# Two destinations in one sum of the count table: weights 1 and 256, and one 16-bit copy for two bytes

## The reference, cut to what matters

```python
pooled = jax.ops.segment_sum(h[col], row, num_segments=N)       # first network, 2 layers
agg    = jax.ops.segment_sum(h[src], dst, num_segments=N)       # second network, 4 layers
agg    = agg / jnp.maximum(deg, 1.0)[:, None]
aggregated = jax.ops.segment_sum(messages, receivers, num_segments=n_nodes)
```

## Time and profile before

| what | value |
|---|---|
| median of 3 runs | 3236.5 us (3234.55 to 3239.82) |
| the profiled execution's span | 3240.8 us |
| TensorE busy | 2943.5 us (91%), mean granted clock 0.951 |
| VectorE busy | 1047.2 us (32%) |
| ScalarE busy | 729.8 us (23%) |
| GpSimd busy | 1114.7 us (34%) |

### The profile page before, as it was taken

How to read it: one execution, slowest core, us unless ns; L and a number is a source line. 1 busy time by engine, 2 the same in 40 slices (tenths; PEclk the granted TensorE clock), 3 DMA queues, 4 the chain that set the end, 5 groups by cost and what they waited for, 6 DMA issues and landing times. The chain is left out here.

```text
span 3240.8 us, 44117 instructions
## 1 busy us (share of the span) xinstructions
PE 2943.5 (91%) x18657; PEld 1740.9 (54%) x18657; DVE 1047.2 (32%) x1860; ACT 729.8 (23%) x1173; POOL 1114.7 (34%) x1012
## 2 busy tenths in 40 slices
PE   1799969997899869999999999999899877999998
PEld 1688835553444335555555555554355664555554
DVE  5899922223200261211111111113311483222122
ACT  4799912223100230000000000001100383011000
POOL 5000013330000004562562663664167101553564
PEclk6899979998999979999999999999899987999999
DMA  7133599994466226666665665664566213665665
GB/s 260 50 129 129 163 244 173 164 170 89 120 147 146 44 66 206 178 171 169 177 175 165 182 178 163 173 173 121 146 181 179 78 54 101 176 180 161 171 170 156
DMA packets 768367, 492.61 MB, mean 152 GB/s; under 512 B 362500, under 2 KB 749836, under 8 KB 767568
## 3 DMA queue, kind: packets, MB, share of 16 engines
q1 hardware_dynamic: 705362, 395.76, 50.5%
q0 software_dynamic: 30112, 62.69, 6.6%
q10 hardware_dynamic: 32702, 31.44, 3.1%
HBM read 334.89 MB, written 76.82 MB: 127 GB/s over the span
## 5 line engine op out<-in xcount | busy, mean ns | idle before, releaser
L2159 PE MATMUL acc<-tbuf,hs 128*128 128x448 fp8e4 x8232 | 1602.0, 354 | 20.0 <-PEq L1242 8.8
L2136 POOL DMA_INDIRECT grow<-hrows,glist x882 | 940.6, 1066 | 791.9 <-PE acc L2183 388.3
L2159 PEld LDWEIGHTS acc<-tbuf,hs 128*128 128x128 f16 x8232 | 801.2, 98 | 762.9 <-issue 52.5
L2298 DVE TENSOR_TENSOR edge_loc<-iota,gdl 128x768 f16<-128x768 bf16 x147 | 140.6, 971 | 743.9 <-PE acc L2183 714.4
L731 PE MATMUL quad<-K,S 128*128 128x196 bf16 x1568 | 278.0, 250 | 17.6 <-DVE K L655 17.6
L1627 PE MATMUL acc<-tbuf,hs 128*128 128x512 fp8e4 (+1 forms) x1300 | 279.6, 369 | 14.9 <-DMA tbuf<-table 14.9
L711 ACT ACTIVATE stage<-quad 128x784 fp8e4<-128x784 f32 x392 | 287.4, 838 | 11.6 <-PE quad L731 5.8
L735 PE MATMUL deg<-K,S 128*128 128x196 bf16 x1568 | 276.8, 248 | 0.0
L1500 PE MATMUL acc<-tbuf,hs 128*128 128x512 fp8e4 (+1 forms) x1300 | 267.4, 369 | 0.7 <-issue 0.7
L2267 ACT ACTIVATE H<-B,vectors 128x448 f32<-128x448 f32 (+2 forms) x56 | 37.4, 668 | 820.3 <-DVE B L2338 820.3
L1500 PEld LDWEIGHTS acc<-tbuf,hs 128*128 128x128 f16 x1300 | 123.6, 98 | 144.4 <-issue 4.3
(11 more groups left out here) (301 smaller groups left out, 2008.5 us busy)
## 6 DMA issues: line engine op xcount, KB each, us to landing
tbuf<-table SPq DMA_DIRECT2D x294, 448.0 KB, 3.6
tbuf<-table SPq DMA_DIRECT2D x294, 336.0 KB, 3.2
table<-stage SPq DMA_DIRECT2D x6, 5488.0 KB, 19.4
grow<-hrows,glist POOLq DMA_INDIRECT x882
hrows<-hs SPq DMA_DIRECT2D x28, 448.0 KB, 4.4
feat<-in_edge_attr_dram ACTq DMA_DIRECT2D x27, 448.0 KB, 6.6
C<-factors ACTq DMA_DIRECT2D x2, 3136.0 KB, 12.5
table<-stage SPq DMA_DIRECT2D x2, 2744.0 KB, 12.2
```

Source lines behind the costliest of these rows:

```text
L2136: g.indirect_dma_start(out=grow[:, n % 2, t, :], out_offset=None, in_=k.hrows[l % 2], in_offset=bass.IndirectOffsetOnAxis(k.glist[:, i // ...
L2159: mm = T.matmul(acc(s, h), rows[l % 2][:, g * US + r, part, :], counts[:, (r - lo) * STRIP + h * HALF:(r - lo) * STRIP + (h + 1) * HALF], ...
L2298: V.tensor_tensor(hot[:, n % 2, :, :], k.iota[:, 0:P].unsqueeze(1).to_broadcast([P, GH, P]), k.gdl[:, i // GU, i % GU * GH:(i % GU + 1) * ...
```

## The change

One sum holds two destinations. A window still has four destinations, but a key now has only two places per block of sources (WU = 2, so NKEY falls from 196 to 98). The lower bit of the destination goes into the weight instead: an edge to an even destination adds 1, one to an odd destination adds 256. So S is no longer a plain one-hot array but a weighted one, and it is written with one instruction per window, which reads two numbers per partition (`win_low` and `win_odd`) as its scalar operands. A sum below 65536 is copied as one 16-bit integer, whose two bytes are the two counts, eight windows per copy. Read as 8-bit floats, the bytes 0 to 15 stand for the count times 2^-9 (CODE), and the scales by which the sums are multiplied take that back. The degrees and the check for large counts take the two bytes apart first. The core of the diff:

```diff
-NKEY = NS * WD
+WU = WD // 2
+NKEY = NS * WU
+ODD = 256.0
+CODE = 2.0 ** -9
-NQUAD = NBATCH * NBW // 4
+NWE = 8
+NOCT = NBATCH * NBW // NWE
...
# first_stage, windows(n)
-                    V.tensor_scalar(high[at], both[:, :, :, 0], 7, None, ALU.logical_shift_right)
+                    V.tensor_scalar(high[at], both[:, :, :, 0], 6, 0xFFFE, ALU.logical_shift_right, ALU.bitwise_and)
+                    V.tensor_scalar(junk[at].bitcast(I32), both[:, :, :, 1], 1, None, ALU.bitwise_and)
...
-                    V.scalar_tensor_tensor(loc[:, 1, g0:g1, :], high[at], float(WD), dl[at], ALU.mult, ALU.add
+                    V.scalar_tensor_tensor(loc[:, 1, g0:g1, :], dl[at], 1.5, high[at], ALU.is_ge, ALU.add
                                            ).then_inc(loc_ok.h, 1)
+                    V.tensor_scalar(loc[:, 2, g0:g1, :], junk[at].bitcast(I32), ODD - 1.0, 1.0, ALU.mult, ALU.add
+                                    ).then_inc(loc_ok.h, 1)
...
# build_tables, VectorE
-                        hot(S[:, q, :, :], k.iota[:, 0:SRC_W], k.win_low[:, at, :], NBW, SRC_W)
+                        for i in range(NBW):
+                            w = u * NBW + i
+                            V.tensor_scalar(S[:, q, i, :], k.iota[:, 0:SRC_W], k.win_low[:, w:w + 1],
+                                            k.win_odd[:, w:w + 1], ALU.is_equal, ALU.mult)
                         hot(K[:, q, :, :], k.iota[:, 0:NKEY], k.win_key[:, at, :], NBW, NKEY).then_inc(hots.h, 1)
...
-                V.tensor_reduce(degl[:, :], deg[:, 0:2 * NKEY].rearrange("p (h b d) -> p b h d", h=2, d=WD), AXY, ALU.add
+                V.tensor_copy(packed[:, :], deg[:, 0:2 * NKEY]).then_inc(split_ok.h, 1)
+                dve.wait_ge(split_ok.h, split_ok.at(1))
+                V.tensor_scalar(bytes_of[:, 0, :], packed[:, :], 255, None, ALU.bitwise_and)
+                V.tensor_scalar(bytes_of[:, 1, :], packed[:, :], 8, None, ALU.logical_shift_right).then_inc(split_ok.h, 1)
+                dve.wait_ge(split_ok.h, split_ok.at(2))
+                V.tensor_tensor(summed[:, :], bytes_of[:, 0, :], bytes_of[:, 1, :], ALU.add).then_inc(split_ok.h, 1)
+                V.tensor_tensor(many[:, :], bytes_of[:, 0, :], bytes_of[:, 1, :], ALU.max).then_inc(split_ok.h, 1)
+                dve.wait_ge(split_ok.h, split_ok.at(4))
+                V.tensor_reduce(degl[:, :], summed[:, :].rearrange("p (h b d) -> p b h d", h=2, d=WU), AXY, ALU.add
                                 ).then_inc(deg_ok.h, 1)
+                V.tensor_reduce(verdict[:, 1:2], summed[:, :], AX, ALU.add).then_inc(judge.h, 1)
...
# build_tables, ScalarE: 196 copies of eight windows in place of 392 of four
-                            stage[:, b, :, to:to + 4 * WD].rearrange("p b (w d) -> p w b d", d=WD),
+                            pairs16[:, b, :, to:to + NWE * WU].rearrange("p b (w d) -> p w b d", d=WU),
...
# build_tables, TensorE: both products of a window are 98 columns wide
+                            mm = T.matmul(pair[o % 3][:, at:at + NKEY], S[:, q, i, :], K[:, q, i, :],
...
# layer_chain, TensorE, ahead of layer 0
+                if conv:
+                    pe.wait_ge(own_ok.h, own_ok.at(2 * L))
...
# layer_chain, VectorE, at the place of L2370
-                if conv:
-                    V.tensor_scalar(own[1][:, :], layers[1][0], scale(0, 1), None, ALU.mult).then_inc(own_ok.h, 1)
+                for l in range(L if conv else 0):
+                    for i in range(2):
+                        V.tensor_scalar(own[l][i], layers[l][0], scale(0, l), (CODE, 1.0)[i], ALU.mult, ALU.mult
+                                        ).then_inc(own_ok.h, 1)
```

More of the change, by code:

```diff
@@ L10 @@
 I32 = mybir.dt.int32
+U16 = mybir.dt.uint16
 ALU = mybir.AluOpType
@@ L567, in lists @@
                 def lists(m):
-                    g0, g1 = WHALF[m // 2]
+                    g0, g1 = WHALF[m // 3]
                     act.wait_ge(loc_T.h, loc_T.at(2 + m))
[L570 to L574, removed]
+                    at = turned[(m + 1) % 4][:, 0:(g1 - g0) * P]
+                    if m % 3 == 0:
+                        return k.win_key[:, g0 * P:g1 * P, :], at.unsqueeze(2).to_broadcast([P, (g1 - g0) * P, 2])
+                    return (k.win_odd if m % 3 == 1 else k.win_low)[:, g0 * P:g1 * P], at
+                for m in (0, 1):
+                    to, at = lists(m)
+                    A.activation(to, at, ACT.Copy).then_inc(loc_out.h, 1)
+                for m in (3, 4):
                     to, at = lists(m)
@@ L577, in _ @@
                 act.wait_ge(judged.h, judged.at(1))
-                for m in (1, 3):
+                for m in (2, 5):
                     to, at = lists(m)
@@ L603, in build_tables @@
         many = sb("many", [P, 2 * NKEY], F32)
+        packed = sb("packed", [P, 2 * NKEY], I32)
+        bytes_of = sb("bytes_of", [P, 2, 2 * NKEY], I32)
+        summed = sb("summed_b", [P, 2 * NKEY], F32)
+        verdict = sb("verdict_b", [P, 4], F32)
         ones = sb("ones_b", [P, 1], F32)
@@ L674, in _ @@
+                V.scalar_tensor_tensor(many[:, :], many[:, :], COUNT_MAX + 0.5,
                                        ones[:, 0:1].to_broadcast([P, 2 * NKEY]), ALU.is_gt, ALU.mult,
-                                       accum_out=k.spilled[:, 1:2]).then_inc(judge.h, 1)
+                                       accum_out=verdict[:, 0:1]).then_inc(judge.h, 1)
                 dve.wait_ge(deg_T.h, deg_T.at(1))
                 V.tensor_copy(degr[:, :], pair[0][0:NS, 0:P]).then_inc(deg_ok.h, 1)
-                dve.wait_ge(judge.h, judge.at(2))
@@ L703, in _ @@
                 A = nc.scalar
+                pairs16 = stage[:, :, :, :].rearrange("p s b c -> p (s b c)").bitcast(U16).rearrange(
+                    "p (s b u) -> p s b u", s=2, u=SU)
                 for h in range(NHALF):
@@ L726, in _ @@
                             w = u * NBW + i
[L727 to L733, removed]
+                            o = w // NWE
+                            if w % NWE == 0 and o >= 3:
+                                pe.wait_ge(moved.h, moved.at(o - 2))
+                            at = w % NWE // (NWE // 2) * 512 + w % (NWE // 2) * NKEY
+                            mm = T.matmul(pair[o % 3][:, at:at + NKEY], S[:, q, i, :], K[:, q, i, :],
+                                          start=(w % (NWE // 2) == 0), stop=True, skip_group_check=True)
+                            if w % NWE == NWE - 1:
                                 mm.then_inc(filled.h, 1)
@@ L739, in _ @@
                 pe.wait_ge(deg_ok.h, deg_ok.at(1))
[L740 removed]
+                pe.wait_ge(moved.h, moved.at(NHALF * NOCT))
                 T.transpose(pair[0][0:NS, 0:P], degl[:, :], k.idf[:, :]).then_inc(deg_T.h, 1)
[L742 to L743 removed]
+                pe.wait_ge(judge.h, judge.at(2))
+                T.matmul(pair[1][:, 0:2], k.avg[:, :], verdict[:, 0:2], start=True, stop=True).then_inc(judge.h, 1)
                 for m in range(4):
@@ L1381, in _ @@
             V = nc.vector
-            scale = k.scales[:, 1, at_scale:at_scale + 1]
+            scale = k.scales[:, 2, at_scale:at_scale + 1]
             dve.sem_inc(acc_read.h, 2)
@@ L2091, in layer_chain @@
             "p (b t c) -> p b t c", b=2, c=P)
-        own = [k.own_scaled] + ([sb("own", [P, D], F32)] if conv else [])
+        own = [[k.W[n] for n in names] for names in (("a0", "a1"), ("b0", "b1"))]
         out_rows = dst[:, :].rearrange("p (b f) -> p b f", f=D)
@@ L2155, in dense_piece @@
                             if conv:
-                                T.matmul(acc(s, h), own[l][:, :], v[:, chunk_of(s, h)], start=True, stop=False)
+                                T.matmul(acc(s, h), own[l][0], v[:, chunk_of(s, h)], start=True, stop=False)
                         for r in range(lo, hi):
@@ L2176, in gathered @@
                         if conv:
-                            T.matmul(to, own[l][:, :], v[:, (GB0 + b) * P:(GB0 + b + 1) * P], start=True, stop=False,
+                            T.matmul(to, own[l][1], v[:, (GB0 + b) * P:(GB0 + b + 1) * P], start=True, stop=False,
                                      skip_group_check=True)
@@ L2789, in program @@
         with ExitStack() as lists:
-            k.win_low, k.win_key = (lists.enter_context(nc.sbuf_tensor(f"win_{n}", [P, NWIN, 2], BF16))
-                                    for n in ("low", "key"))
+            k.win_low, k.win_odd = (lists.enter_context(nc.sbuf_tensor(f"win_{n}", [P, NWIN], BF16))
+                                    for n in ("low", "odd"))
+            k.win_key = lists.enter_context(nc.sbuf_tensor("win_key", [P, NWIN, 2], BF16))
             first_stage(k, w["x"], w["src"], w["dst"], small_loads(k, w))
```

58 lines of the change are left out of this document (32 added, 26 removed).

## The result

The changed kernel takes 3383.86 us (3381.08 to 3385.93, 4 runs), the kernel before 3235.72 us on the same chips: ratio 1.0453, 95% interval 1.0439 to 1.0468, slower. The prediction was 3384 us, +147 us; measured were +148.1.

A forecast was written before the change was run, and what follows sets the result against it. VectorE was taken to bound the table stage: 142.5 there plus 0.6, 0.5, 3.5 and 0.2 made +147 us on a 3240.8 us span, 3388; run median 4.3 lower, 3384 us. Own range 3365 to 3405, overall 3340 to 3440.

The forecast's parts named there:

- The stage's length decides, and VectorE sets it: Table stage, 112 batches: VectorE takes 3.91 us per batch, so the stage is 441 us in place of 298.7, +142.5 us.
- small terms: Outside the table stage's main loop: windows +0.6, stage's end +0.5, last network's scaled weights +3.5, two more scalings +0.2 us.
- S: 33 ns of stream and 190 of gap: Table stage, VectorE: each of 14 S instructions per batch costs 223 ns start to start, 3.12 us per batch.
- the loop's share: Unknown hardware-loop part of the 190 ns gap read from L1138's two-scalar instructions; 73 and 190 ns were the ends.
- the tiny instructions: Short VectorE instructions in no loop: 0.15 us without a scalar from memory, 0.21 with one; used to support 190 ns.
- K: 0.79 us: Table stage, VectorE: the half-wide K of 1372 elements costs 0.709 us of stream plus 0.08 us per batch.
- TensorE and ScalarE hide behind it: Table stage: TensorE at most 3.7 us and ScalarE 1.29 us per batch, both behind VectorE's 3.91 us.
- the bound of 3.7: Table stage, TensorE: 28 products at 0.133 us at the lower clock, at most 3.7 us per batch.
- the third rival: Table stage: TensorE stays at 1.2 GHz, 0.15 us per product, 4.2 us per batch; +180 us, 3416 us; chance 4%.
- The rival on the other side: Table stage: scalars from memory cost nothing, S 106 ns, batch 2.27 us, stage 258 us, 3200 us in all; chance 6%.

The follow-up runs named there:

- the wider instruction: Changed kernel with S as seven 256-column instructions per batch instead of 14 of 128, every second window taking its neighbour's source and weight: 3234.9 us.
- the run with the later clearing: Changed kernel with GpSimd's clearing of grow in the last network made to wait until VectorE has scaled the four weights: 3382.7 us.
- the run in which GpSimd multiplies: Against the kernel before: weights multiplied onto K instead of S, GpSimd multiplying 6 of 14 windows per batch, later clearing of grow: 3306.5 us, ratio 1.0208.
- the run in which VectorE multiplies alone: Against the kernel before: S and K by one instruction each, a third on VectorE multiplying K by the weights, later clearing of grow: 3231.3 us, ratio 0.9987.
- sharing it with ScalarE: Against the kernel before: weights multiplied onto K, ScalarE multiplying 3 of the 14 windows of each batch: 3215.4 us, ratio 0.993.

## Why the prediction was right, point by point

- **The stage's length decides, and VectorE sets it.** Right: 142.2 of 143.1 us in the spans lie between the stage's first S and its last copy. That 3384 us was met to 0.2 us is luck: the four runs spread over 4.9 us, and the sum itself was 147 us on spans that came to differ by 143.1. The measured stage and small terms add up to 145.9 us; the 3.2 us in the layers between take the spans' difference down to 142.7, and 0.4 us came elsewhere.
- **S: 33 ns of stream and 190 of gap.** Right in the sum (223 forecast, 223.6 measured) and in both parts, which the change alone could not have shown: 33.5 ns by the wider instruction, 61 ns for each scalar and 69 for the rest (102 less the stream) by taking the scalars away. The prediction had 117 for the two scalars and 73 for the rest. It had to choose 190 ns without knowing the loop's share; the tiny instructions on which it leaned had one scalar only. The durations were not forecast well: 0.30 us were expected for one S and 0.337 measured, so two neighbours overlap by 113 ns where the strips of the earlier trace rows overlap by 86. Only the distances from start to start made the sum. Why the duration is longer is open.
- **K: 0.79 us.** 0.78.
- **TensorE and ScalarE hide behind it.** Right. A batch of 28 products takes about 2.46 us at the lower clock (62.60 us for 712 products, 88 ns each), under the bound of 3.7. The fall of the clock that the third rival rested on did come, for the whole stage, but not its price: at 88 ns in place of 150 for a product, VectorE's 3.91 us covered it.
- **The rival on the other side.** Scalars from memory are not free. The estimate by the errata figure of the Trainium skill's "VectorE: DVE Perf Modes" (94 ns for S, 775 for K) was near for K (783 ns) and for an S without scalars (102 ns); the figure has no term for scalars, and these were the loss.
- **Small terms.** The first stage +0.5 (0.6 forecast; the `win_low` copies start 1.86 us later and are 1.38 us shorter), the stage's end 0 (0.5), the last network +3.25 (3.5). The cause of the last was the one named, as the run with the later clearing shows.

## What to carry to other kernels

When several engines are level in a stage, an edit that relieves two of them is priced on the third, in distances from start to start. One wide two-input instruction that becomes many short ones with scalars from memory paid here a fixed gap of 69 ns and 61 ns for each scalar, at 128 columns together nearly six times the stream itself. A weight that can't be had in the same instruction was cheaper here as one more wide product, with a share of it on the engine that the change had relieved.

## What the runs showed of the hardware that was not expected

- TensorE's clock level differed between runs with the same products. The stretch from 200 to 300 us with no scalar, with one, and with S twice as wide:

```profile
200.00:300.00 100.00, 63.73 (x1272) 57.12 (x1273) 100.00 (x681) 63.12 (x79) 0.00 (x0) 1.00 0.51 165
200.00:300.00 100.00, 61.86 (x922) 56.11 (x920) 100.00 (x493) 47.44 (x58) 0.00 (x0) 0.76 0.35 114
200.00:300.00 100.00, 68.73 (x1073) 62.42 (x1074) 100.00 (x310) 54.74 (x67) 0.00 (x0) 0.81 0.44 141
```

  The level was 1.00 at 2.21 us per batch, 0.76 on the mean at 3.06 and 0.81 at 2.59, against 0.50 at 3.91 in the changed kernel, while TensorE's busy share was 62 to 69% in all four. What moved the level is not shown.
- The row of the granted clock can mislead. In the run in which GpSimd multiplies, at 3.24 us per batch, it reads 1.00, yet a product lasts as long as in the changed kernel at 0.50 (284 and 283 ns), not as in the run without scalars (206 ns). The stretch and the group of products in that run, then the group without scalars:

```profile
200.00:300.00 100.00, 76.19 (x867) 69.56 (x866) 100.00 (x93) 45.69 (x54) 60.33 (x31) 1.00 0.35 114
L779 PE MATMUL deg<-K,S 128*128 128x98 bf16 x1568 | 269.5, 284 | 0.0
L768 PE MATMUL deg<-K,S 128*128 128x98 bf16 x1568 | 153.2, 206 | 0.0
```

- A GpSimd instruction on two tensors and a VectorE instruction on two tensors took turns: 1.45 us for a product that alone takes an estimated 0.49. Set against the run in which VectorE multiplies alone (each by its chip's kernel before), sharing the work with GpSimd cost 75 us, and sharing it with ScalarE gained 14.
